# Decoder kernel, layer 4: where the key mask of the maxima is put into PSUM

## The reference, cut to what matters

```python
logits = jnp.einsum('bqhd,bkhd->bhqk', q, k) / jnp.sqrt(dh)
neg = (1.0 - mask.astype(q.dtype)) * -1000000000.0
logits = logits + neg[:, None, :, :]
attn = jax.nn.softmax(logits, axis=-1)
attn = attn * group_prob[:, None, :, :]
out = jnp.einsum('bhqk,bhkd->bqhd', attn, v)
```

## Time and profile before

| | us |
|---|---|
| median of three runs | 1508.32 (1502.15 to 1515.01) |
| the profiled execution | 1505.13 |
| its span, first to last instruction | 1503.4 |
| mean granted clock of TensorE | 0.968 |
| busy share of the span: TensorE, VectorE, ScalarE, GpSimd | 95%, 66%, 58%, 37% |

### The profile page before, as it was taken

How to read it: one execution, slowest core, us unless ns; L and a number is a source line. 1 busy time by engine, 2 the same in 40 slices (tenths; PEclk the granted TensorE clock), 3 DMA queues, 4 the chain that set the end, 5 groups by cost and what they waited for, 6 DMA issues and landing times. The chain is left out here.

```text
span 1503.4 us, 29009 instructions
## 1 busy us (share of the span) xinstructions
PE 1430.2 (95%) x11096; PEld 1077.9 (72%) x11096; DVE 994.6 (66%) x2109; ACT 877.6 (58%) x1442; POOL 558.5 (37%) x727
## 2 busy tenths in 40 slices
PE   8999999999989999999999999999999999868997
PEld 5667656666668888888888888865655555437997
DVE  4677777766674455464544534587778989856896
ACT  1455667666646565564645646454547767637775
POOL 4246765613331111321312112152223554442766
PEclk9899999999979999999999999998999999988999
DMA  7689776754450203201010010124765643106451
GB/s 153 100 146 183 148 158 118 136 102 61 67 71 2 43 2 57 36 16 44 2 43 24 21 50 1 44 75 112 135 158 105 118 90 66 38 32 211 143 178 63
DMA packets 100200, 125.98 MB, mean 84 GB/s; under 512 B 7900, under 2 KB 90083, under 8 KB 97504
## 3 DMA queue, kind: packets, MB, share of 16 engines
q1 hardware_dynamic: 96496, 118.84, 38.4%
q0 software_dynamic: 1984, 4.09, 0.8%
q10 hardware_dynamic: 1584, 1.20, 0.3%
HBM read 50.96 MB, written 9.51 MB: 40 GB/s over the span
## 5 line engine op out<-in xcount | busy, mean ns | idle before, releaser
L950 ACT ACTIVATE probs<-eslot 128x1024 f32<-128x1024 f32 x188 | 192.6, 1024 | 110.0 <-PE eslot L682 106.6
L1174 DVE TENSOR_REDUCE mx<-mslot 128x4 f32<-128x1024 f32 x128 | 156.4, 1222 | 108.7 <-PE mslot L653 107.3
L1473 POOL TENSOR_SCALAR_AFFINE_SELECT probs<-probs 128x512 f32<-128x512 f32 x128 | 82.6, 646 | 352.3 <-ACT probs L948 351.7
L653 PE MATMUL mslot<-stack 48*128 48x256 f32 (+2 forms) x1110 | 166.2, 338 | 8.7 <-DVE mx L1174 5.9
L653 PEld LDWEIGHTS mslot<-stack 48*128 48x128 f32 (+1 forms) x1110 | 99.3, 191 | 96.9 <-issue 76.6
L1168 DVE TENSOR_REDUCE mx_blocks<-mslot 128x3 f32<-128x384 f32 x214 | 114.7, 554 | 60.3 <-PE mslot L653 44.9
L948 ACT ACTIVATE probs<-eslot 128x512 f32<-128x512 f32 (+1 forms) x256 | 111.7, 490 | 43.5 <-PE eslot L682 43.1
L697 PE MATMUL bank<-probs,v 128*32 128x256 f32 (+1 forms) x2048 | 133.0, 373 | 2.2 <-ACT slot_rows_sb L973 0.8
L1412 POOL TENSOR_SCALAR ave<-amv 128x2 f32<-128x2 f32 x64 | 22.7, 355 | 293.1 <-DVE amv L1086 252.4
L682 PE MATMUL eslot<-stack 50*128 50x256 f32 (+1 forms) x1264 | 125.3, 276 | 5.0 <-ACT probs L950 2.4
L745 PE MATMUL bank<-slot_rows_sb,l 128*128 128x256 f32 x512 | 114.8, 382 | 0.0
(11 more groups left out here) (277 smaller groups left out, 3488.7 us busy)
## 6 DMA issues: line engine op xcount, KB each, us to landing
stack<-split SPq DMA_DIRECT2D x192, 256.0 KB
w<-in_w SPq DMA_DIRECT2D x16, 1024.0 KB, 6.2
stack<-split SPq DMA_DIRECT2D x96, 128.0 KB
slot_rows_sb<-in_proj SPq DMA_DIRECT2D x15, 256.0 KB, 3.8
slot_rows<-hTf SPq DMA_DIRECT2D x4, 650.0 KB, 4.5
slot_rows_sb<-slot_rows SPq DMA_DIRECT2D x4, 650.0 KB, 5.2
expert_rows<-slot_rows SPq DMA_DIRECT2D x8, 260.0 KB, 2.7
hT<-in_xT SPq DMA_DIRECT2D x8, 256.0 KB, 9.5
```

What stands on the lines that cost most here:

```text
L653: mm = pe.matmul(ps[:, first:first + m], queries(u, h, k)[:, qt * P:(qt + 1) * P], keys(u, h, k)[:, 0:m], start=clear, stop=clear or qt == ...
L950: e = act.activation(PR[:, k, :, :, :].rearrange("p a k q -> p (a k q)"), ps[:, :, :, :].rearrange("p a k q -> p (a k q)"), ACT.Exp, scale ...
L1174: dve.tensor_reduce(MX[:, :, :, p].rearrange("p q a -> p a q"), MSLOT[0][:, :, :].rearrange("p a (q k) -> p a q k", q=TT), AX.X, ALU.max)\
L1473: pool.affine_select(diagonal, diagonal, [[0, 2 * TT], [1, P]], ALU.is_ge, 0.0, base=0, channel_multiplier=-1)\
```

## The change

For units 33 to 38 the mask of the maxima is no longer put into PSUM by TensorE. ScalarE copies `NQ` into the two banks of `MSLOT[0]` in one instruction (128 x 1024, bf16 to f32), one slot ahead of the scores; TensorE adds the scores to it, without start. The wait for VectorE's reading of the previous pair and the wait for the mask tile move from TensorE to ScalarE, and TensorE waits for the copy.

```diff
@@ schedule()
             if l in MASKED:
-                if u not in MASK_ADDED:
+                if u in MASK_SEEDED:
+                    put(at(p) - 1, EXP, "max seed", u, p)
+                elif u not in MASK_ADDED:
                     put(at(p), MASK, "max mask", u, p)
@@ scores_for_max(u, p), TensorE
             clear = l not in MASKED or u in MASK_ADDED
+            if u in MASK_SEEDED:
+                pe.wait_ge(*act_step.at("max seed", u, p))
+                for a in range(2):
+                    last_in_max[max_bank(u, p, a)] = u, p, a
...
-                                   skip_group_check=l in CAUSAL)
+                                   skip_group_check=l in CAUSAL or u in MASK_SEEDED)
@@ ScalarE
+        def seed_maxima(u, p):
+            if p == 0:
+                act.wait_ge(*pool_step.at("nk", u))
+            act.wait_ge(*(maxima_read(u, p - 1, 1) if p else maxima_read(u - 1, PAIRS - 1, 1)))
+            neg = NQ[u % RING].rearrange("p a s -> p (a s)").unsqueeze(1).to_broadcast([P, 2, TT * S])
+            act.activation(MSLOT[0][:, :, :], neg, ACT.Copy).then_inc(*act_step("max seed", u, p))
...
+            elif step == "max seed":
+                seed_maxima(u, n)
```

## The result

The changed kernel takes 1532.41 us (median of four runs, 1529.56 to 1536.10) where the kernel before, run beside it, takes 1511.66 (four runs, 1502.15 to 1516.16); the ratio is 1.0147, with a 95% interval of 1.0087 to 1.0207. It is slower, as forecast, by 20.8 us in the medians; the forecast of 1535 us is 2.6 us off. The profiled execution has a span of 1527.7 us against 1503.4, so +24.3.

The account below looks back on a forecast made before the run. TensorE was taken to set the pace (96% busy), with VectorE close behind; the change would close a chain through ScalarE. Terms 25.6 - 2.5 + 3.5 = +26.6 us gave 1531.7 on the profiled execution, forecast 1535 us, range 1520 to 1554.

Parts of the forecast that it names:

- slot E: Fifth of a layer 4 sequence's eight slots (A first); forecast 5.66 us, mix waiting for a read behind the copy.
- A to D: First four slots of a layer 4 sequence, the ordinary ones; forecast 4.08 us each, 16.32 together.
- TensorE stays the bound: Rival: the copies fit in ScalarE's free time and all 25.4 us come back, 1480 to 1483 us; chance 0.06.
- 48 slots: Layer 4 slots that lose TensorE's mask matmuls and get ScalarE's copy; 25.4 us to gain if TensorE stayed the bound.
- The closed chain: Layer 4: maxima, exponent scores, exponentials, seed, copy, next maxima wait on each other in a round of 4.08 us a slot.
- E, F, G, H: Last four slots of a layer 4 sequence, with ScalarE's other work; forecast 5.66, 4.08, 4.56 and 5.38 us.
- The eleven slots: Layer 4 slots 263 to 273, with the copy as only seed; forecast 37.4 against 39.90 us, -2.5.
- the five short ones settle at 3.02: Among slots 263 to 273, those of 2.36 to 3.25 us were to take 3.02, a chain one seed shorter.
- The clock: TensorE's gaps in layer 4 lower its granted clock; one dip of 0.7 us in each of five sequences, +3.5 us.
- 37 slots: Layer 4 slots 274 to 310, where ScalarE runs both seeds; forecast 164.2 against 138.58 us, +25.6.
- The rival of a clock that falls for most of the stretch: Rival: TensorE's clock dips in every slot with both seeds, +52 us, 1557 to 1560 us; chance 0.12.

Follow-up runs that it names:

- second measurement: The changed kernel measured and traced once more without any edit, beside the kernel before: ratio 1.0116, 1524.30 us beside 1509.39.
- copy_first: The changed kernel with ScalarE making the copy for the maxima ahead of the seed of the exponents: ratio 1.0097 to the kernel before.

## Why the prediction was right, point by point

*What bounds the kernel.* TensorE set the pace of the ordinary slots, as I read it from the earlier trace rows. But it did not set slot E in the third, fourth and last sequence: GpSimd did. I had not asked why the first two of these slots take 6.8 us where the second sequence has 5.4. For the forecast this did no harm, as the lengthened A to D hid the wait; for the rival "TensorE stays the bound" it did. Its 25.4 us were not to be had: leaving the matmuls out altogether gives 6.5 us in the 48 slots.

*The closed chain.* Right in every link, too long by 0.13 us: 4.08 forecast, 3.95 measured. Two links account for it. From the scores to the exponentials I took 0.63 from the earlier trace rows, a slot in which the scores themselves had been held up; with a free run it is 0.52, which the earlier trace rows already had (1166.97 to 1167.49). The copy takes 1.01, not 1.03. In this kernel the copy is 0.58 us at 512 columns and 1.01 at 1024, 0.84 ns a column with 0.15 us besides. The Trainium skill, "ScalarE: Activation LUTs", section "What ACT_TABLE_LOAD costs", gives 0.833 ns a column and 186 ns besides for an instruction with immediate scale and bias, with back-to-back instructions overlapping by 93 ns; the trace agrees nearly (0.15 us, and a next instruction 0.95 us after a start).

*The slots with other work.* Without a dip of the clock (second measurement, last whole sequence) E, F, G, H take 5.47, 4.04, 4.55, 5.00 us; the forecast was 5.66, 4.08, 4.56, 5.38. The walk through ScalarE's reads holds, the bank wait of slot E with it, and H grew most (3.44 before), as forecast. A sequence was forecast at 36.00 and takes 35.36 to 35.77, dips included. Wrong was slot E of the last sequence: 5.66 forecast, 3.94 measured. I had carried over the bank assignment of the others, though two steps of a next unit (`q` and `q end`) are missing there: the mix starts 1.7 us ahead of the read L904 in the trace and does not wait for it.

*The eleven slots.* -2.5 forecast, +0.7 measured, and -0.2 in the second trace (nearly all of the difference is slot 266, 3.70 and 2.89 us; the clock of the eleven was 0.96 and 1.00). The step that failed is "the five short ones settle at 3.02": I left out of these slots what I had counted in G, the turned maxima with their DMA and the reads behind them. The count was off as well, with little effect: by the starts of L653 six of the eleven are under 3.25 us, not five. Slot 265 went from 2.36 to 3.74 us; the exponentials (L956) start 1.74 us after the maxima at 1095.18, behind these:

```profile
1095.06 0.36 ACT L1037 ACTIVATE mT<-bank 32x256 fp32r<-32x256 f32 x1
...
1096.19 0.84 ACT L937 ACTIVATE split<-bank,cols 128x256 fp32r<-128x256 f32 x2 [0.77 <-ACT mT L1037]
1096.92 1.02 ACT L956 ACTIVATE probs<-eslot 128x1024 f32<-128x1024 f32 x1
...
1097.83 1.04 ACT L980 ACTIVATE mslot<-l 128x1024 f32<-128x1024 bf16 x1
```

*The clock.* The mechanism came, near its forecast size. The granted clock of the 37 slots is 0.93 (0.95 in the second trace), 1.00 before. In windows of 4 us:

```profile
1166.00:1170.00 4.00, 3.68 (x40) 1.76 (x32) 2.30 (x4) 3.14 (x5) 1.37 (x1) 0.80 1.14 167
1170.00:1174.00 4.00, 2.71 (x28) 1.67 (x28) 3.03 (x6) 3.57 (x5) 2.93 (x3) 1.00 1.13 141
1190.00:1194.00 4.00, 3.82 (x26) 2.57 (x30) 2.62 (x8) 3.31 (x6) 0.00 (x0) 0.69 0.02 4
...
1278.00:1282.00 4.00, 4.00 (x24) 2.52 (x28) 1.67 (x2) 2.78 (x3) 3.38 (x5) 0.50 1.15 145
```

At 1278 TensorE ran at 1.2 GHz (0.50) for the whole window, in slot C of the last sequence, which took 5.04 us instead of 3.95. Counting the slots above the length that their like have at full clock (D of the third sequence +0.9, G and H together +0.5 in the second and again in the fourth, C and D of the last +1.4, A and B of the second +0.3) gives 3.6 us; I had put 3.5. For slot G of the second sequence (6.09 us at a clock of 0.73) beside that of the third (4.56 at 1.00) the matmuls themselves show it:

```profile
1191.28 1.70 PE L548 MATMUL bank<-slot_rows_sb 128*128 128x256 f32 x4
1192.91 0.64 PE L722 MATMUL bank<-probs,sum_cols 128*32 128x256 f32 x1
...
1227.60 1.03 PE L548 MATMUL bank<-slot_rows_sb 128*128 128x256 f32 x4
1228.56 0.40 PE L722 MATMUL bank<-probs,sum_cols 128*32 128x256 f32 x1
```

The first takes 0.67 us longer, and the mix takes 1.86 instead of 1.00 to the next L659 (1194.77 and 1229.56), together the 1.53 by which the slots differ; the next slot H is then 0.98 shorter, as ScalarE had done most of its other work by then. For the other slots the cause follows from the place of the dips alone: no run held the clock fixed. The rival of a clock that falls for most of the stretch did not come: the first sequence ran 33.38 us at 1.00 with a gap ahead of the maxima in nearly every slot. So the section of the Trainium skill that the prediction named for this rival ("TensorE: Matmul & The Clock Gate", "A second HAM failure mode: psum-queue depth-cycling") describes what happens here in kind, not in extent.

*The sum.* Forecast 25.6 - 2.5 + 3.5 = 26.6, measured +24.3 in the span. The term of the 37 slots with its clock, 29.1, came to 22.9, of which the 0.13 us a slot make 4.8 and slot E of the last sequence 1.7; the term of the eleven was 3.2 too low. Part of the closeness is luck. These two errors have opposite signs. And the 2.6 us between 1535 and the measured median flatter the forecast: it set +26.6 on a kernel before of 1508.32, and the medians measured side by side differ by 20.8 (1511.66 to 1532.41), in the second measurement by 14.9.

## What to carry to other kernels

When engines hand a single buffer round, add up the links of the whole round and compare the sum with the period before counting anyone's free time: ScalarE had 39.4 us free here, yet 0.43 us off the round was 0.43 us off every ordinary slot. Before moving an operation, ask whether it is needed, and price its removal by itself: here it was worth 6.5 us, not 25, in these 48 slots, and 16.4 once the next chain, over GpSimd, was shortened too.

## What the runs showed of the hardware

- From the end of ScalarE's write in PSUM to the first matmul that waited for it the traces show 0.05 to 0.06 us (1175.18 to 1175.23; 1209.97 to 1210.03 with half the copy).
- The seed, which waits for the end of the exponentials because it overwrites their banks, starts 1.06 us after they began (1172.15 to 1173.21); the copy, which does not, starts 0.92 after them in `copy_first` (1206.51 to 1207.43). With the copy between them that link of the round is 0.14 us shorter.
- Gaps of TensorE of about 1.1 us in slots of 3.95 us went with a full clock for 33 us on end (1129.67 to 1163.05), and with 0.50 for 4 us elsewhere in the same layer (1278 to 1282). Which slots fall was nearly the same in two executions.
